# A recurrent scan and attention block: who loads the first x chunk and stores the last results, and how the scan's weights are prepared

## The reference

```
m = concat(x_t, h) @ weight + bias           # weight 256 x 256: rows 0..127 for x, 128..255 for h
h = g * h + (1 - g) * c,  g = sigmoid(m[:, :128] + 1), c = tanh(m[:, 128:])
```

## Time and profile before

| What | Value |
|---|---|
| Median of 3 runs | 463.29 us (462.67 to 463.84) |
| Span of the profiled execution | 461.8 us, no other time is given for it |
| Median less this span | 1.5 us |
| PE busy | 375.0 us (81%) |
| DVE busy | 304.8 us (66%) |
| ACT busy | 231.7 us (50%) |
| POOL busy | 78.5 us (17%) |

### The profile page before, as it was taken

How to read it: one execution, slowest core, us unless ns; L and a number is a source line. 1 busy time by engine, 2 the same in 40 slices (tenths; PEclk the granted TensorE clock), 3 DMA queues, 4 the chain that set the end, 5 groups by cost and what they waited for, 6 DMA issues and landing times.

```text
span 461.8 us, 14117 instructions
## 1 busy us (share of the span) xinstructions
PE 375.0 (81%) x5296; PEld 253.9 (55%) x5296; DVE 304.8 (66%) x1938; ACT 231.7 (50%) x1025; POOL 78.5 (17%) x151
## 2 busy tenths in 40 slices
PE   1999899898857896857898999979599899778832
PEld 1755676566746675746666766636344446446510
DVE  5454444576777776777776676653842378699883
ACT  2123422325335425335446455645688878953952
POOL 7000000012000012000012000032210124266580
PEclk9999999999999999999999999985759989995966
DMA  7200840002000000000000000000000000000102
GB/s 179 62 1 4 181 95 3 2 3 48 1 1 3 1 4 1 2 2 1 2 3 3 1 4 1 2 2 2 3 2 3 1 2 4 1 2 1 23 1 68
DMA packets 9114, 8.42 MB, mean 18 GB/s; under 512 B 1276, under 2 KB 7694, under 8 KB 9047
## 3 DMA queue, kind: packets, MB, share of 16 engines
q1 hardware_dynamic: 8950, 7.26, 7.0%
q0 software_dynamic: 96, 0.26, 0.2%
HBM read 6.45 MB, written 1.08 MB: 16 GB/s over the span
## 4 chain that ended last, share of the span: by engine, by line
PE 56%; DVE 22%; ACT 12%; issue 5%; POOL 2%; DMA 1%; SPq 0%; DVEq 0%; ACTq 0%; POOLq 0%
PE zb L804 21%; PE tb L927 6%; PE zb L782 4%; DVE prod_hi L1569 4%; PE tb L751 4%; ACT state L1265 3%; PE firsts L1098 3%; PE firsts L983 2%; ACT prd L1421 2%; PE tb L898 2%; PE zb L1078 2%; PE firsts L967 2%; ACT state L1268 2%; PE zb L788 2%; PE firsts L804 2%
## 5 line engine op out<-in xcount | busy, mean ns | idle before, releaser
L804 PEld LDWEIGHTS zb<-prod_hi,whh 128*128 128x128 f16 x1920 | 73.7, 106 | 89.9 <-DVE prod_hi L1569 85.8
L1265 ACT ACTIVATE state<-zb 128x8 f32<-128x8 f32 x240 | 42.7, 178 | 152.9 <-PE zb L804 152.4
L804 PE MATMUL zb<-prod_hi,whh 128*128 128x8 f16 x1920 | 91.0, 171 | 34.7 <-DVE prod_hi L1569 34.0
L1569 DVE SCALAR_TENSOR_TENSOR prod_hi<-state 128x16 f16<-128x16 f32 x255 | 44.7, 175 | 83.0 <-ACT state L1268 80.1
L804 PE MATMUL zb<-prod_lo,whh 128*128 128x8 f16 x960 | 63.7, 172 | 0.0
L1575 DVE TENSOR_TENSOR prod_lo<-prod,prod_hi 128x16 f16<-128x16 f32 x255 | 44.7, 175 | 8.7
L1421 ACT ACTIVATE prd<-zb 128x640 f32<-128x640 f32 x64 | 42.2, 712 | 7.8 <-PE zb L1078 7.2
L804 PEld LDWEIGHTS zb<-prod_lo,whh 128*128 128x128 f16 x960 | 44.5, 107 | 0.8
L1571 DVE SCALAR_TENSOR_TENSOR prod<-state 128x16 f32<-128x16 f32 x256 | 43.3, 169 | 0.3 <-ACT state L1268 0.3
L1268 ACT ACTIVATE state<-zb 128x16 f32<-128x16 f32 x240 | 42.8, 178 | 0.0
L1577 DVE SCALAR_TENSOR_TENSOR state<-prod 128x8 f32<-128x8 f32 x256 | 40.8, 159 | 0.0
(11 more groups left out here) (378 smaller groups left out, 708.6 us busy)
## 6 DMA issues: line engine op xcount, KB each, us to landing
mod<-ada_rows SPq DMA_DIRECT2D x4, 768.0 KB, 11.8
resid<-in_x_dram SPq DMA_DIRECT2D x6, 128.0 KB, 3.7
ffz<-shift_rows SPq DMA_DIRECT2D x4, 131.0 KB, 3.3
out_dram<-state SPq DMA_DIRECT2D x8, 64.0 KB, 2.1
out_dram<-early SPq DMA_DIRECT2D x8, 64.0 KB, 2.1
yy<-in_L_cond_w_ada_dram SPq DMA_DIRECT2D x1, 384.0 KB
early<-in_L_cond_weight_dram SPq DMA_DIRECT2D x2, 128.0 KB
resid<-in_x_dram POOLq DMA_DIRECT2D x2, 128.0 KB, 3.5
```

The lines of the kernel that those rows point to most:

```text
L804: i = pe.matmul(z_bank(t, k)[:, NB * (t % CH):NB * (t % CH) + NB], whh[:, half, p, k, :], src[:, NB * p:NB * p + NB], start=False, stop=Fa ...
L1265: act.activation(r[:, 24:32], z_bank(t, 1)[:, k:k + NB], ACT.Tanh, scale=-1.0 / ZS)
L1569: dve.scalar_tensor_tensor(prod_hi[:, :], r[:, 16:32], 1.0, r[:, 0:16], ALU.add, ALU.mult).then_inc(hi_ready, 1)
```

## The change

- x chunk 0 is issued by ACT at its start (`load_tiles(act, 0, load_x0)`), no longer by POOL.
- ACT, no longer SP, issues the stores of the last pair (j = 3), at the end of its stream, each two behind `last_out`.
- POOL writes only the zeros of V. The ones column of V (value `C_HEAD`) and the zeros of O are written by ACT at ticks 14, 16 and 18 of the scan; attention waits for them (`act_init`) at its first group, near tick 197.
- DVE works on the bias first, writes the high part of the recurrent weights directly out of the loaded weights, and makes the low part with four fused multiply-subtract instructions; the buffer `whs` is gone.
- PE transposes x chunk 0 before it waits for `load_scan`; `first_x_part` adds the bias before x. `copy_xT(0)` is cut in two: 16 steps, then 48, with the copies of the condition between them.

```diff
-            for slot in range(2):
-                tile_dma(pool, x, resid, 0, slot, False).then_inc(load_x0, 16)
...
-            settled(pool.memset(V[:, :, :, :, :], 0.0))
-            pool.memset(V[:, :, :, :, HD:HD + 1], C_HEAD)
-            pool.memset(O[:, :, :, (NC - 1) * P:NC * P], 0.0).then_inc(pool_init, 1)
+            pool.memset(V[:, :, :, :, :], 0.0).then_inc(pool_init, 1)
...
             def first_x_part():
 
                 n = NB * FIRST
-                for k in range(2):
-                    pe.matmul(z_bank(0, k)[:, 0:n], w0s[:, k, :], xT[:, 0:n], start=True, stop=False,
-                              skip_group_check=True)
+                pe.wait_ge(x_split, 1)
+                for k in (1, 0):
                     for half in range(2):
                         pe.matmul(z_bank(0, k)[:, 0:n], b0h[:, half, k, :], onesh[:, 0:n],
-                                  start=False, stop=False, skip_group_check=True)
+                                  start=(half == 0), stop=False, skip_group_check=True)
+                pe.wait_ge(xT_sb, 1)
+                for k in (1, 0):
+                    pe.matmul(z_bank(0, k)[:, 0:n], w0s[:, k, :], xT[:, 0:n], start=False, stop=False,
+                              skip_group_check=True)
...
-            pe.wait_ge(load_scan, 64)
             pe.wait_ge(consts, 1)
-            transpose(tb[:, 0, 0:NB], condr[:, :], identf).then_inc(condT_ps, 1)
             for _ in x_transposes(0):
                 pass
-            pe.wait_ge(x_split, 1)
-            pe.wait_ge(xT_sb, 1)
+            pe.wait_ge(load_scan, 64)
+            transpose(tb[:, 0, 0:NB], condr[:, :], identf).then_inc(condT_ps, 1)
             first_x_part()
...
+            load_tiles(act, 0, load_x0)
...
+            copy_xT(0, 0, FIRST)
             act.wait_ge(condT_ps, 1)
...
-            copy_xT(0)
+            copy_xT(0, FIRST, CH)
...
             def prepare(now):
+                for q in range(2):
+                    yield from at_ticks(now, 14 + 2 * q)
+                    act.activation(view(O[:, 2 * q, 0, (NC - 1) * P:(NC - 1) * P + 1], [NC * P, 4], [1, P]),
+                                   view(identf[:, 0:1], [0, 4], [1, P]), ACT.Copy, scale=0.0)
+                yield from at_ticks(now, 18)
+                act.wait_ge(pool_init, 1)
+                act.activation(V[:, :, :, :, HD:HD + 1].rearrange("p b k h a -> p (b k) (h a)"),
+                               view(identf[:, 0:1], [0, 2 * NB], [1, NH]),
+                               ACT.Copy, scale=0.0, bias=C_HEAD).then_inc(act_init, 1)
...
             run(step, [prepare, tokens, attention, *tails])
+            for par in range(2):
+                act.wait_ge(last_out, par + 1)
+                store_tiles(act, NJ - 1, par)
...
-            for k, off in ((0, D), (1, 0)):
-                s = ZS * (1.0, 0.5)[k]
-                dve.tensor_scalar(w0s[:, k, :], w0x[:, off:off + D], s, None, ALU.mult)
-                dve.tensor_scalar(whs[:, 0, k, :], w0h[:, off:off + D], s / 4, None, ALU.mult)
-                dve.tensor_scalar(whs[:, 1, k, :], w0h[:, off:off + D], s / 2, None, ALU.mult)
+            parts = ((0, D, ZS), (1, 0, ZS * 0.5))
+            for k, off, s in parts:
                 done_(dve.tensor_scalar(b0s[:, k, :], b0row[:, off:off + D], s, (0.0, s)[k],
                                         ALU.mult, ALU.add))
-            settle()
-            settled(dve.tensor_copy(b0h[:, 0], b0s[:, :, :]))
-            dve.tensor_tensor(b0h[:, 1], b0s[:, :, :], b0h[:, 0], ALU.subtract).then_inc(x_split, 1)
-            settled(dve.tensor_copy(whh[:, 0], whs[:, :, :, :]))
-            dve.tensor_tensor(whh[:, 1], whs[:, :, :, :], whh[:, 0], ALU.subtract).then_inc(w_split, 1)
+            mark = done[0]
+            for k, off, s in parts:
+                dve.tensor_scalar(w0s[:, k, :], w0x[:, off:off + D], s, None, ALU.mult)
+            settle(mark)
+            done_(dve.tensor_copy(b0h[:, 0], b0s[:, :, :]))
+            mark = done[0]
+            for k, off, s in parts:
+                for p in range(2):
+                    done_(dve.tensor_scalar(whh[:, 0, p, k, :], w0h[:, off:off + D], s / (4, 2)[p], None,
+                                            ALU.mult))
+                if k == 0:
+                    settle(mark)
+                    dve.tensor_tensor(b0h[:, 1], b0s[:, :, :], b0h[:, 0], ALU.subtract).then_inc(x_split, 1)
+            for n, (k, off, s) in enumerate(parts):
+                for p in range(2):
+                    settle(mark + 1 + 2 * n + p)
+                    i = dve.scalar_tensor_tensor(whh[:, 1, p, k, :], w0h[:, off:off + D], s / (4, 2)[p],
+                                                 whh[:, 0, p, k, :], ALU.mult, ALU.subtract)
+            i.then_inc(w_split, 1)
```

More of the change, by code:

```diff
@@ L513, in ugrnn_block_kernel, with load_tiles, store_tiles @@
         block = ctx.enter_context(nc.Block())
[L516 to L521, removed]
+        def load_tiles(eng, c, sem):
+            par = c % 2
+            for slot in range(2):
+                rows = bass.AP(x.tensor, ((slot ^ par) * STEPS + CH * c) * D,
+                               [[D, CH], [2 * STEPS * D, NJ], [1, D]])
+                eng.dma_start(resid[CH * slot:CH * slot + CH, NJ * c:NJ * c + NJ, :], rows).then_inc(sem, 16)
+        def store_tiles(eng, j, par):
+            for slot in range(2):
+                rows = bass.AP(out.tensor, (batch_of(par, j, slot) * STEPS + CH * par) * D,
+                               [[D, CH], [2 * CH * D, NC // 2], [1, D]])
+                eng.dma_start(rows, T_R[j][CH * slot:CH * slot + CH, par:NC:2, :]).then_inc(stored[j], 16)
         def row(ap):
@@ L568, in _ @@
                                          [[0, CH], [2 * ZW, NJ], [1, ZW]])).then_inc(zsh_in, 16)
-            for j in range(NJ):
-                if j < NJ - 1:
-                    sp.wait_ge(res_ready, j + 1)
+            for j in range(NJ - 1):
+                sp.wait_ge(res_ready, j + 1)
                 for par in range(2):
[L574 to L581, removed]
+                    store_tiles(sp, j, par)
             for j in range(NJ):
@@ L779, in x_part @@
                     for q in range(1 if c == 0 else 0, 4):
-                        if k == 0 and c and q == 0:
-                            pe.wait_ge(xT_sb, c + 1)
+                        if k == 0 and q == (0 if c else 1):
+                            pe.wait_ge(xT_sb, c + 2)
                         pe.matmul(zb[:, c % 2, k, 128 * q:128 * q + 128], w0s[:, k, :],
@@ L1244, in settled, with copy_xT @@
                 act.wait_ge(act_done, done[0])
+            load_tiles(act, 0, load_x0)
+            def copy_xT(c, t0=0, t1=CH):
+                act.wait_ge(xT_ps, c + 1)
+                first = xT[:, NB * (CH * c + t0) + batch_of(c, 0, 0):][:, 0:1]
+                s = batch_of(c, 0, 1) - batch_of(c, 0, 0)
+                act.activation(view(first, [2, NJ], [s, 2], [NB, t1 - t0]),
+                               xT_bank(c).rearrange("p (j s t) -> p j s t", j=NJ, s=2)[:, :, :, t0:t1],
+                               ACT.Copy).then_inc(xT_sb, 1)
+            copy_xT(0, 0, FIRST)
             act.wait_ge(condT_ps, 1)
@@ L1249, in _ @@
             act.activation(condT[:, :], tb[:, 0, 0:NB], ACT.Copy).then_inc(condT_sb, 1)
[L1251 to L1254, removed]
-                act.activation(view(first, [2, NJ], [s, 2], [NB, CH]),
-                               xT_bank(c).rearrange("p (j s t) -> p j s t", j=NJ, s=2),
-                               ACT.Copy).then_inc(xT_sb, 1)
-            copy_xT(0)
+            copy_xT(0, FIRST, CH)
             def step(t):
```

11 lines of the change are left out of this document (5 added, 6 removed).

## The result

| | before | changed |
|---|---|---|
| median | 463.56 us (4 runs, 462.67 to 464.15) | 455.47 us (4 runs, 454.85 to 456.59) |
| ratio | | 0.983, 95% interval 0.9814 to 0.9847 |
| profiled execution: span | 461.8 us | 453.1 us |
| first tanh of the scan | 13.66 us | 9.35 us |
| first tanh to last tanh | 281.90 us | 281.70 us |

The change saves 8.1 us, 1.7%. The prediction was 457.5 us with a range of 456.0 to 460.3: the sign is right, the gain of 5.8 us is too small, and the time lies outside the range. The profile divides the span into four parts; in these two executions they give 4.31, 0.20, 1.88 and 2.31 us, together 8.70. Spans are given to 0.1 us, so the part behind the last arithmetic is good to 0.05 us.

What follows compares the result with a forecast made beforehand. The prediction took the chain of waits as the bound, with gains only at the two ends: 3.2 us at the start plus 2.6 at the end, 5.8 off 463.3, gave 457.5 us, range 456.0 to 460.3.

Steps and rivals of the forecast that it cites:

- What bounds the start: Start of the kernel: POOL's memsets hold DVE's weight scalings, so DVE is free at 9.61 us, not at 5.24.
- the size of the start: Start: step 0 on PE moves from 13.27 to 10.12 us, a gain of 3.15, taken as 3.2.
- The chunk's issue began at 1.26; I take that.: POOL's start: its first memset moves from 2.76 to 1.26 us, so V is done at 6.60.
- They are the same eight in another order: PE's x and bias matmuls ahead of step 0: 2.17 us, the same after the reordering.
- PE sets the start: Step 0: PE is ready at 10.12 us, 0.20 behind DVE's signal at 9.92, so PE decides.
- upper bound for the gain of the start: Start: a gain of 4.0 us at most, with POOL beginning at 0.44.
- rival of late weights: Start: weights land at 7.78 us and 1.18 is lost, time 458.7; chance 0.12 together with a 6 us clock stretch.
- The three writes: ACT's writes at scan ticks 14, 16 and 18: priced at 0, at worst 0.9 us for three.
- The end: Last stores: SP and ACT issue side by side, SP is last at 457.32 us, a gain of 2.57.
- transfers as the bound: Last eight stores: transfers or a common issuer set the pace, no gain at the end, time 460.1 us; chance 0.11.
- The 1.5 us that I added: Outside the span: the median of the runs lies 1.5 us over the profiled span, kept unchanged.
- rival of the granted clock: PE behind the scan: clock stretches change; 6 us either way is 2 us; chance of it turning against the change 0.04.

Runs made afterwards that it cites:

- e2: The kernel before, with x chunk 0 issued by ACT instead of POOL and nothing else changed; 460.66 us, ratio 0.9942 to before.
- e7: The changed kernel with one more memset, of half of V, ahead of POOL's first one; 458.44 us, ratio 0.9888 to before.
- e8: The changed kernel, but POOL's memset of V waits until DVE has split the weights; 459.77 us, ratio 0.9916 to before.
- e12: The kernel before, with POOL's three memsets behind the signal of step 0 and attention's wait for them at its first group; 460.32 us.
- e10: The changed kernel, but POOL's memset of V waits for the signal of step 0 and runs beside the first scan steps; 454.20 us.
- e11: The changed kernel, with PE's first x part in the order of before (x, then bias, for each half); 455.68 us.
- e3: The kernel before, with the last pair's stores issued by ACT and nothing else changed; 461.02 us, ratio 0.9941 to before.
- e5: The kernel before, with only DVE's preparation of the weights taken from the changed kernel; 462.30 us, ratio 0.999 to before.
- e9: The changed kernel again in more runs, without any edit; 455.06 us, ratio 0.983 to before.
- e13: The changed kernel again without any edit, beside another kernel on the same chip; 455.72 us, ratio 0.9842 to before.
- e6: The changed kernel with one more memset, of all V, ahead of POOL's first one; 458.93 us, ratio 0.9905 to before.

## Why the prediction was too small

**What bounds the start: right.** POOL's memsets hold DVE's scalings. e2, e7 and e8 move the memset and the hold moves with it, to within 0.13 us, and e12 takes it away by one wait. The section "SBUF: two separate sides" of the page "SBUF — State Buffer" of the Trainium skill says that of a DVE operation in a 2-port mode and a GpSimd operation, the one that starts first has the port pair which they share for its whole instruction, and that a GpSimd operation which doesn't read SBUF isn't in the way of a DVE instruction with two SBUF inputs. The traces agree: one-source scalings and casts were held for up to 3.9 us, and the fused two-source instructions beside the same memset took 0.17 us (e10). In which mode an instruction ran the traces don't show.

**The step that failed: the size of the start, 1.16 us too small.** I predicted a gain of 3.15 us at step 0; in PE's timeline it moved from 13.20 to 8.89, and the first tanh from 13.66 to 9.35, both 4.31. (The predicted 10.12 counts from the chain's 13.27; the chain has step 0 at 9.03 now.) Three terms of the sum make up the 1.16:
- "The chunk's issue began at 1.26; I take that." POOL's memset began at 0.72. The 1.26 is the start of a DMA issue and not of a memset; V was done at 6.01 and not at 6.60, 0.59 us. It lay inside the bounds that I gave (0.44 to 1.76).
- DVE's way from there to the bias split took 1.21 and not 1.3, 0.09.
- "They are the same eight in another order": from the bias split to step 0 PE took 2.15 in the timeline before (11.05 to 13.20) and 1.67 now (7.22 to 8.89), 0.48 less. e11 puts the old order back and step 0 comes 0.48 later. A reordering was priced at nothing because the instructions were the same.

That the third term came out in full took a fourth error on the same side: the four fused instructions needed 0.88 us and not 1.22, so DVE's signal came 1.60 behind the bias split and not 2.02. "PE sets the start" no longer holds with the new order: the profile has PE idle for 0.15 us until DVE's signal at 8.82, and step 0 stands 0.07 behind it, as in e8, where PE waited for that signal for 3.58 us. It is DVE's signal that releases step 0 now.

My upper bound for the gain of the start, 4.0, failed as well (4.31): it varied only the moment at which POOL begins. With the start as predicted the time would have been 456.6, inside the range.

**The loads: right.** The weights landed at 4.78, earlier than before, with x chunk 0 on ACT's queue ahead of them. The rival of late weights did not come.

**The three writes: right**, 0.63 and 0.68 us in idle time of 0.81, priced at 0.

**The end: right.** 2.31 for 2.57: the issues side by side take 0.66 to 0.68 each (SP's four 0.15 us more than predicted), and the landing 2.0 us (0.11 more). The rival (transfers as the bound, 460.1) falls with e3 and a DMA share of 0.65, where I had estimated 0.84.

**What was not in the sum.** Over all runs the medians of the spans are 461.2 (45 runs) and 453.55 (14 runs), 7.65 apart: start 4.31, end 2.31, step 27 of the scan 0.31 (e12: ACT's stream), and 0.72 in the rest of the middle. Outside the span come 0.31 more, since time less span is 2.13 in the kernel before and 1.82 in the changed one. (The 1.5 us that I added was the median time less one span that happened to be long; what matters is that I took it as unchanged.) In the experiments time less span is 1.79 to 1.89 in every kernel with the new preparation on DVE, e5 with it alone included, and 2.12 to 2.14 in every other. So it comes with DVE's part. Why, the profile doesn't show.

**Open.** Of the 0.72 us left in the middle I can show only that the middle scatters, and that it does so in two places. Behind the scan, three profiled executions of the changed kernel (the first, e9, e13) took 157.57, 158.38 and 159.52 us, at mean granted clocks of 0.87, 0.86 and 0.82. The scan itself took 281.70, 280.69 and 281.03 us in the same three, spread over most of its steps, and no row here says why. Medians of four to six runs of kernels with the same instructions in the middle lie between 439.4 and 441.3. The changed kernel's 439.7 over 14 runs against 440.75 - 0.31 = 440.4 over 45 may be that scatter or an effect of the moment at which the tails begin; no run here separates them. My rival of the granted clock was of the right size for a stretch ("6 us, either way, is 2 us") and it is a scatter of one kernel, not an effect that I could have put on one side.

**The range** failed by 0.5 us because its low end (456.0) allowed for little beyond the likeliest case on the fast side, though 2 us of clock stood beside it and its own upper bound for the start was too low. About 1.3 us of the gain (step 27, the time outside the span, the rest of the middle) lay in places where the sum had put nothing.

## What to carry to other kernels

When an instruction takes ten times its usual length, compare its end with the ends of the other engines' instructions, not with its own start: two ends 0.1 us apart named POOL's memset, and the best version here (e10) runs that memset beside two-source instructions. After taking such a hold away, look at every one-source instruction that the moved work can now meet (e8), and at the next path in line (e12). At the end of a kernel, count issue times: here stores queued on one engine cost 0.64 us each, and two engines' queues worked side by side at a DMA share of 0.65.

## What the runs showed of the hardware that was not expected

- A cast of 128x16 on DVE took 3.90 us beside a memset of POOL that it met at its start, and a fused instruction of the same size 0.17 us beside the same memset (e8, e10).
- POOL's first memset can start at 0.72 us, but an issue of a DMA by POOL only at 1.26, and two such issues keep POOL from its memsets until 2.76.
- One step of the scan is 0.31 us longer or not by what stands in ACT's stream (1.45 against 1.13), at whatever moment it comes (e12).
- The time outside the span of the profile is 2.13 us in some kernels and 1.8 in others, by the code of DVE's start (e5).
- The same 1583 matmuls of attention and tails take from 157.2 (e11, mean granted clock 0.87) to 159.8 us (e8, 0.85) in the profiled executions; the lowest mean clock, 0.82, gave 159.5 (e13). So the mean clock alone does not order them.
- The hold works both ways: an instruction of POOL that takes 0.29 us took 1.31 beside DVE's scalings (e6).
- PEclk reads 1.00 for all of the start and the scan, yet a matmul of 128x128 float32 takes there what it takes at 0.50 in the tails, and not what it takes at 1.00. Four lines of the changed kernel, from the views of L745 and L1133 in windows where PEclk reads 1.00, 1.00, 0.50 and 1.00 (shortest/median/longest in ns, first and last start in us):

```profile
L745 PE MATMUL tb<-identf,resid x4: 421/421/448, 5.2 to 5.9; 128*128 128x128 f32 x4
L745 PE MATMUL tb<-identf,tw x4: 421/438/474, 107.2 to 108.8; 128*128 128x128 f32 x4
L1133 PE MATMUL firsts<-gw,xT x8: 421/421/421, 416.3 to 417.7; 128*128 128x128 f32 x8
L745 PE MATMUL tb<-identf,xT x4: 272/273/299, 420.9 to 421.3; 128*128 128x128 f32 x4
```

By these rows TensorE works at 1.2 GHz in the start and the scan. So PEclk of 1.00 in those two stretches is no sign of full speed, and the mean clocks given above for the stretch behind the scan may be a little too high.
